# Identity matmuls into a spare PSUM bank in TensorE's waits of one language-model block

## What is computed

```python
x = emb[tokens] * sqrt(256) + pos_enc
h = softmax(q k^T / sqrt(256), axis=1) @ v                 # per row of 256 tokens
h = h + mixer(layernorm(h))                                # layernorm, in_proj, conv of 4 taps, silu,
                                                           # chunked scan, gate, rms norm, out_proj, residual
scores = softmax(layernorm(h) @ w_router); top 2 of 8      # capacity 1024 slots an expert
y[e] = gelu(xb[e] @ w1[e]) @ w2[e]                         # xb[e]: the 1024 token rows of expert e
h = h + scatter_add(weights * y) + bias
```

## Time and profile before

| | |
|---|---|
| median of 3 runs | 974.99 us (973.57 to 975.16) |
| the profiled execution | 972.38 us, its span 970.6 us |
| TensorE busy | 893.6 us, 92% of the span |
| VectorE, ScalarE, GpSimd busy | 634.4, 529.2, 493.9 us |
| chain of waits, share of TensorE | 80% |
| mean granted clock of TensorE | 0.96 of full speed |

### The profile page before, as it was taken

The page is one execution under the profiler, slowest core; times in us unless marked ns, Lnnn a source line. Parts: engine busy times, 40 slices in busy tenths (PEclk is TensorE's granted clock), DMA queues, the critical chain, the costliest instruction groups (busy, mean ns, idle before and its releaser), DMA issues.

```text
span 970.6 us, 17232 instructions
## 1 busy us (share of the span) xinstructions
PE 893.6 (92%) x5580; PEld 790.1 (81%) x5580; DVE 634.4 (65%) x1665; ACT 529.2 (55%) x1094; POOL 493.9 (51%) x491
## 2 busy tenths in 40 slices
PE   5699999999999999999998629999999999999992
PEld 4588888888888888888886419999999999999992
DVE  3477898888988898888986333636463636363620
ACT  1467777677677767677665123545444544444330
POOL 2157776887678777887677221232333232323322
PEclk9899999999999999999997659999999999999996
DMA  7920111001000000000000034344343433342121
GB/s 228 325 63 6 39 38 40 22 33 32 12 22 17 19 13 24 22 13 23 12 22 13 13 100 137 70 106 94 81 107 71 108 71 103 71 108 29 21 24 22
DMA packets 49038, 57.58 MB, mean 59 GB/s; under 512 B 6208, under 2 KB 44715, under 8 KB 49008
## 3 DMA queue, kind: packets, MB, share of 16 engines
q1 hardware_dynamic: 34992, 41.23, 13.3%
q0 software_dynamic: 14016, 15.97, 10.7%
HBM read 33.09 MB, written 29.75 MB: 65 GB/s over the span
## 4 chain that ended last, share of the span: by engine, by line
PE 80%; DVE 10%; issue 3%; DMA 2%; POOL 2%; SPq 1%; ACT 1%; DVEq 0%; POOLq 0%
PE bank L1536 12%; PE bank L1538 12%; PE bank L1537 12%; PE bank L1334 11%; PE bank L1443 5%; PE bank L1279 4%; PE bank L1424 4%; PE bank L1318 3%; PE bank L1300 3%; PE bank L1309 3%; PE bank L1293 2%; PE bank L1396 2%; DVE seg L1019 2%; PE bank L1458 2%; PE bank L1548 2%
## 5 line engine op out<-in xcount | busy, mean ns | idle before, releaser
L627 POOL DMA_INDIRECT out<-ye,tok_slot x64 | 110.7, 1730 | 286.0 <-DMA out<-ye,tok_slot 155.2
L837 ACT ACTIVATE hf<-bank 128x512 f32<-128x512 f32 x128 | 79.3, 619 | 203.6 <-PE bank L1538 203.6
L1232 DVE TENSOR_TENSOR h_lo<-hf,h_hi 128x512 fp32r<-128x512 f32 x128 | 88.7, 693 | 104.7 <-ACT h_hi L839 104.7
L1536 PE MATMUL bank<-w_hi,h_hi 128*128 128x256 f32 x512 | 146.1, 285 | 0.0
L1537 PE MATMUL bank<-w_lo,h_hi 128*128 128x256 f32 x512 | 144.9, 283 | 0.0
L1538 PE MATMUL bank<-w_hi,h_lo 128*128 128x256 f32 x512 | 144.9, 283 | 0.0
L991 DVE SCALAR_TENSOR_TENSOR xc<-bank,cw,xc 128x253 f32<-128x253 f32 (+2 forms) x288 | 128.2, 470 | 1.7
L1536 PE MATMUL bank<-xe_hi,w_hi 128*128 128x512 f32 x256 | 100.9, 394 | 2.7 <-DVE xe_lo L1224 2.7
L1537 PE MATMUL bank<-xe_lo,w_hi 128*128 128x512 f32 x256 | 100.5, 393 | 0.0
L1538 PE MATMUL bank<-xe_hi,w_lo 128*128 128x512 f32 x256 | 100.4, 392 | 0.0
L578 POOL DMA_INDIRECT slots_dram<-rows,slot x64 | 63.4, 990 | 71.8 <-DVE slot L1120 57.2
(11 more groups left out here) (200 smaller groups left out, 2289.7 us busy)
## 6 DMA issues: line engine op xcount, KB each, us to landing
w_raw<-w SPq DMA_DIRECT2D x16, 1024.0 KB, 8.3
slots_dram<-zero_row SPq DMA_DIRECT2D x1, 8320.0 KB, 29.9
xe<-slots_dram SPq DMA_DIRECT2D x16, 520.0 KB, 4.7
out<-hb SPq DMA_DIRECT2D x16, 256.0 KB, 2.1
w_raw<-in_wT SPq DMA_DIRECT2D x1, 1288.0 KB, 8.9
slots_dram<-rows,slot POOLq DMA_INDIRECT x64, 2.2
out<-ye,tok_slot POOLq DMA_INDIRECT x64, 3.8
xg<-emb,idx POOLq DMA_INDIRECT x36, 3.9
```

The lines of the kernel that those rows point to most:

```text
L627: g.indirect_dma_start(out, bass.IndirectOffsetOnAxis(ap=tok_slot[q][:, j:j + 1], axis=0), ye[q][:, j, :], None, compute_op=ALU.add).then_ ...
L837: sc.activation(hf[m % 2][:, :], h_bank[i % H_BANKS][:, :], ACT.Gelu_apprx_tanh)\
L1232: vc.tensor_tensor(h_lo[:, m, :], hf[m % 2][:, :], h_hi[:, m, :].bitcast(F32), ALU.subtract)\
L1536: te.matmul(out_, hi, rhi, start=first_, stop=False)
```

## The change

`keep_clock(spare, times)` issues `times` matmuls of the 128x128 f32 identity by itself into the first 128 columns of bank 1 of a set that is not in use. Nobody reads them and they signal nobody. They stand at these places of TensorE's queue:

- ahead of the kernel's first matmul, once the identity is made (12), and after the product of the query and key weights (2);
- in the first half, where only `f` exists (`FILL`: 3, 2, 4, 16, 7);
- in the drain (`DRAIN`: 2, 3, 4, 4, 3, 2, 2, 2, 2, 2, 2) and in the last half (`LAST`: 18, 2, 8);
- between the last half and the experts: 26 ahead of the wait for `part_done`, 14 behind it, and 8 after the first `turn_x`.

The loops over the turns and over the experts hold none. Otherwise the order is the same. The wait for the masks moves ahead of the one for the early loads.

```diff
+        FILL = {'t': 3, 'scores': 2, 'attend': 4, 'hT': 16, 'dt': 7}
+        DRAIN = {'state': 2, 'seg0': 3, 'seg1': 4, 'v2T': 4, 'seg2': 3, 'seg3': 2, 'own': 2, 'yT0': 2, 'yT1': 2, 'out': 2}
+        LAST = {'v2T': 18, 'route': 2, 'choices': 8}
...
+            def keep_clock(spare, times):
+
+                for _ in range(times):
+                    te.matmul(bank[spare][1][:, 0:P], ident[:, :], ident[:, :], start=True, stop=True)
+
+            pe.wait_ge(s_masks, 1)
+            keep_clock(1, 12)
             pe.wait_ge(s_early, 16 * N_EARLY)
-            pe.wait_ge(s_masks, 1)
...
                 q = 1 - p
+                filling, draining = not b and not t, not f
+
+                if filling:
+                    keep_clock(q, FILL["t"])
                 if f:
                     query_side(f, p)
...
+                if filling:
+                    keep_clock(q, FILL["attend"])
                 if f:
                     attend(f, p)
+                if draining:
+                    keep_clock(p, DRAIN["v2T"] if b else LAST["v2T"])
                 if t:
                     to_v2T(t, p)
...
+                if b and draining:
+                    keep_clock(p, DRAIN["seg3"])
                 if b:
                     segment_sums(b, q, 3)
                     chunk_state(b, q)
+                if b and draining:
+                    keep_clock(p, DRAIN["own"])
+                if b:
                     own_chunk(b, q, 0)
+                if filling:
+                    keep_clock(q, FILL["hT"])
                 if f:
                     to_hT(f, p)
                 if b:
                     from_state(b, q)
+                if draining and not b:
+                    keep_clock(p, LAST["choices"])
                 if t:
                     choices_before(t, p)
+                if b and draining:
+                    keep_clock(p, DRAIN["own"])
                 if b:
                     own_chunk(b, q, 1)
+                if b and draining:
+                    keep_clock(p, DRAIN["yT0"])
+                if b:
                     to_yT(b, q, 0)
+                if filling:
+                    keep_clock(q, FILL["dt"])
                 if f:
                     project_dt(f, p)
...
+            keep_clock(1, 2)
             to_xT(Turn(1), 0)
...
+            keep_clock(0, 26)
             pe.wait_ge(part_done, 1)
             pe.sem_inc(y_psum, Y0)
+            keep_clock(0, 14)
...
                 if last is None:
                     turn_x(0)
+                    keep_clock(0, 8)
                     return
```

More of the change, by code:

```diff
@@ L1479, in half @@
                     project_z(b, q, 1)
+                if filling:
+                    keep_clock(q, FILL["scores"])
                 if f:
                     scores(f, p)
+                if b and draining:
+                    keep_clock(p, DRAIN["state"])
                 if b:
@@ L1486, in half @@
                     values(f, p)
+                if b and draining:
+                    keep_clock(p, DRAIN["seg0"])
                 if b:
                     segment_sums(b, q, 0)
+                if b and draining:
+                    keep_clock(p, DRAIN["seg1"])
+                if b:
                     segment_sums(b, q, 1)
+                if filling:
+                    keep_clock(q, FILL["attend"])
                 if f:
                     attend(f, p)
+                if draining:
+                    keep_clock(p, DRAIN["v2T"] if b else LAST["v2T"])
                 if t:
@@ L1495, in half @@
                     x_to_rows(b, q, 1)
+                if b and draining:
+                    keep_clock(p, DRAIN["seg2"])
+                if b:
                     segment_sums(b, q, 2)
+                if draining and not b:
+                    keep_clock(p, LAST["route"])
                 if t:
                     route(t, p)
+                if b and draining:
+                    keep_clock(p, DRAIN["seg3"])
                 if b:
@@ L1520, in half @@
                     project_channels(f, p, 1)
+                if b and draining:
+                    keep_clock(p, DRAIN["yT1"])
                 if b:
@@ L1524, in half @@
                     project_channels(f, p, 2)
+                if b and draining:
+                    keep_clock(p, DRAIN["out"])
                 if b:
                     project_out(b, q)
+            keep_clock(1, 2)
             to_xT(Turn(1), 0)
```

## The result

| | before | after |
|---|---|---|
| median of the runs beside each other | 974.28 us (4) | 965.80 us (4) |
| ratio, 95% interval | 1 | 0.9914 (0.9891 to 0.9937) |
| profiled execution, its span | 972.38, 970.6 us | 966.81, 965.1 us |
| TensorE busy in the span | 893.6 us | 914.9 us |
| mean granted clock | 0.96 | 0.982 |

What follows compares the result with a forecast made beforehand. TensorE was taken as the bound mostly at full clock, with gains only in slow-clock stretches where the chain of waits runs through it. 2.3 + 5.4 - 1.2 + 3.0 = 9.5 us off 974.99 gave 965.4 us, range 961.5 to 970.5.

Steps and rivals of the forecast that it cites:

- The price of an identity: Anywhere on TensorE: two records, 0.22 us at full clock, 0.43 us at the lower level, nothing while inside a wait.
- Start: First half, 46 identities: clock held through 33.5 us, speeding later matmuls and transposes, 2.3 us gained.
- the lower bound: Start: gain of only 1.0 us if the clock falls in up to 3.2 us idle before L1318.
- VectorE's bound: Start: the row maximum begins at 23.59 us when VectorE finishes its preparation, so earlier TensorE speedups buy nothing.
- Drain: 28 identities: TensorE's path from 524.07 to 538.32 us runs at full clock, 6.8 us less; six unhidden identities leave 5.4 us.
- Last half: 28 identities: 18 leave 3.5 us idle before the transposes, the clock falls, later identities overrun; 1.2 us lost.
- Boundary: Last half to experts, 48 identities: clock up for eight transposes (0.9 us) and the first product (2.1 us), 3.0 us gained.
- the prediction's own sign of being wrong: Clock falling in the drain, or identities ahead of L1318, L1343 or the first product with nothing idle behind them.
- (1): Last half: clock held there too, +1.3 us instead of -1.2, total 963.0 us; chance 22%.
- (2): Boundary: clock not up at the first product, 3.0 us lost and 0.75 us added, total 969.2 us; chance 12%.
- (3): Drain: clock falls anyway near 524 us, 5.4 us gain becomes 2.6 us loss, total 973.4 us; chance 11%.
- (4): All parts: identities do not hold the clock and overflow their waits, 13.7 us slower, 988.7 us; chance 5%.

Runs made afterwards that it cites:

- the second profile of before: The unchanged kernel before, profiled in a second execution: 975.15 us.
- the drain alone: The change with only the drain's 28 identities kept, none at start, last half or boundary: 970.23 us, ratio 0.9969 to the kernel before.
- the bridged kernel: The change with longer identity groups filling the waits at start, last half and boundary to their end: 960.61 us, ratio 0.9878 to the kernel before.

## Why the prediction was right, and where it was not

The time was forecast at 965.4 us and measured at 965.8. The mechanism (the clock held in the waits, worth something only where the chain of waits goes through TensorE) came out in the start and the drain, and the last half lost what was forecast. The boundary came out otherwise, and luck in the choice of the base made up for it. Step by step:

- **The price of an identity**: 0.22 us at full clock and 0.43 at the lower level. Measured 0.22 (x68, the 34, in 7.59 us from 536.95 to the transposes at 544.54 us) and about 0.44 (x16 in 3.55 us, 549.38 to 552.93).
- **Start**: 2.3 us forecast, 1.0 us as the lower bound, for a fall ahead of L1318. The pair of profiles has just that fall, near 25.8 us, and 1.45 us at the drain, of which 0.64 us is VectorE's earlier readiness and not the identities'; so the pair lies at 0.8 us, below the bound. The fall costs 1.7 us (3.69 against 2.01 us in the chain of waits) and not up to 1.3. But the kernel before can pay for it too, and like for like the start gave 2.3 us (without VectorE's 0.57) and 2.9 us, and 2.6 us in the timed runs of this part: the forecast's 2.3 agrees with them, and the lower bound compared two different cases. VectorE's bound did not stand still at 23.59 us, it was 22.95 in this execution. That L1303 was 1.76 us faster at 14.03 us bought nothing, as forecast; the second profile of before has that product fast without any identity.
- **Drain**: 5.4 us forecast, 5.4 us in the profile (5.36), with six identities in the path and the residual still behind rms. The timed runs of the drain alone gave 3.0 us (1.3 to 4.8). Against the second profile of before 4.1 us of the 5.3 reached the end, since the first product of the experts came to full clock later; the rest is open.
- **Last half**: a loss of 1.2 us behind the transposes, because project_out gains more than rms and 18 identities do not reach to the end of the longer wait. Measured 6.40 - 5.16 = 1.24 us, the clock down at 544.6 us. The near agreement has some luck in it: the forecast left out of its sum the 0.16 us by which its two identities overrun their wait (with them it is 1.4 us), and it did not have the 0.4 us that VectorE's norm took longer ahead of the transposes. Leaving the group out shortened the way from transposes to choices by the same 1.2 us.
- **Boundary**: 3.0 us forecast, 0.3 in the profile and 2.4 in the timed runs of this part alone. This step was mis-sized. I had taken the 14 at the lower level, 6.0 us, so that they end as the rows arrive. The 26 before them had brought the clock up and it was still up 3.12 us later, so the 14 took 3.1 us and left 3.6 us idle; the clock fell in those, the transposes gained nothing (0.9 us forecast), and the eight identities overran VectorE's split by 0.4 us. That is the prediction's own sign of being wrong, identities ahead of the first product with nothing idle behind them. The first product gave its 2.0 us. The largest single loss was no matter of the clock: xe landed 1.1 us later after its issue than in the profile of before (4.77 against 3.66 us; 4.90 in the change's second profile, and at most 3.78 in the bridged kernel's). Why is open. Without it this profile would have 1.5 us here.

So the sum came out by the first pair of profiles at 5.6 us and not 9.5. The medians beside each other moved by 8.5 us (974.28 to 965.80): the median of before lay 1.9 us above its profile there, and the profile of after 1.0 above its median. The forecast took its 9.5 us from 974.99 us, the median of three earlier runs, which lay 0.7 us higher still (974.99 less 9.5 is 965.5; 965.4 was put down). That base made up for the boundary's error by luck. The two profiles of each kernel give 5.5 to 10.3 us between the spans, depending on which are paired. Timed again, the change gave 6.2 us (3.7 to 8.7), an interval that leaves the 9.5 out; the first timing, 8.4 us (6.1 to 10.6), holds it.

Of the rivals, (1), the clock held in the last half, became true when the wait was filled. (2), the clock not up at the first product, was half right: it was down for the transposes and the eight identities, and up from about the product's first matmul. (3), a fall in the drain, was refuted. (4), identities do not hold the clock, was refuted for full columns and came about with narrow ones.

## What to carry to other kernels

Read the granted clock beside the busy time, and fill a wait up to its end. In the last half the clock fell in the 3.6 and 3.7 us that a group left open, in both profiles, and at the boundary in one of two. The work and the fillers behind it ran at double price. Other open rests of 2.65, 3.12 and 3.26 us were survived, so a single profile does not tell what a half-filled wait is worth. With 8 moving columns the fillers did not keep the clock here, with 128 they did, as matmuls or as f32 transposes. A wait to be filled is the one that stands in the changed kernel: it is longer than the old one where the work before it got faster and its releaser did not. And before a profile is compared with another, look for the steps that differ between two profiles of the same kernel.

## What the runs showed of the hardware

- 8-column matmuls with 128x128 weights keep TensorE at 21.97 of 22 us busy and the clock at 0.50; 128-column ones or f32 transposes in the same places hold it at 1.00.
- The clock row of the page of before reads 9 in its first slice, 24 us, although eight matmuls took 3.75 us at 14.54 us and eight of the same size 1.99 us at 26.31 us; durations are the better witness.
- The kernel before spread over 6.7 us in 25 runs beside each other (968.9 to 975.6 us); four versions with filled waits, one of them timed twice, spread over 0.8 to 2.6 us, in 2 to 5 runs each.
- The middle of the kernel, at a granted clock of 1.00 and with the same instructions, took 472.1 to 474.2 us from one profile to the next; no run shows why.
